# The first two graph pairs of an attention layer, normalised and turned at the end of the layer before it

## The reference

```python
h = jnp.maximum(_layernorm(x, axis=-1), 0.0)
x = x + _L0_gnn_ref(h, adj, ...)      # relation, masked by adj, divided by its norm
h = jnp.maximum(_layernorm(x, axis=-1), 0.0)
x = x + _L1_gnn_ref(h, ..., adj)      # additive attention
h = jnp.maximum(_layernorm(x, axis=-1), 0.0)
x = x + _L2_gnn_ref(h, adj, ...)      # norm_adj @ (h @ weight) + bias
h = jnp.maximum(_layernorm(x, axis=-1), 0.0)
x = x + _L3_gnn_ref(h, adj, ...)      # attention with 8 heads of 32, masked by adj

# _L3_gnn_ref
q = (x @ Wq + bq).reshape(b, n, H, HD)
k = (x @ Wk + bk).reshape(b, n, H, HD)
v = (x @ Wv + bv).reshape(b, n, H, HD)
scores = jnp.einsum('bqhd,bkhd->bhqk', q, k) / jnp.sqrt(jnp.float32(HD))
scores = scores + (1.0 - adj)[None, None, :, :] * -1000000000.0
attn = jax.nn.softmax(scores, axis=-1)
out = jnp.einsum('bhqk,bkhd->bqhd', attn, v).reshape(b, n, d)
return out @ Wo + bo
```

## Time and profile before

| | |
|---|---|
| median of 3 runs | 755.95 us (754.49 to 757.42) |
| profiled execution | 755.72 us |
| its span, first to last instruction | 753.8 us |
| mean granted TensorE clock | 0.989 |
| busy PE | 709.9 us (94%) |
| busy DVE | 627.1 us (83%) |
| busy ACT | 564.8 us (75%) |
| busy POOL | 474.5 us (63%) |

### The profile page before, as it was taken

The page is one execution under the profiler, slowest core; times in us unless marked ns, Lnnn a source line. Parts: engine busy times, 40 slices in busy tenths (PEclk is TensorE's granted clock), DMA queues, the critical chain, the costliest instruction groups (busy, mean ns, idle before and its releaser), DMA issues.

```text
span 753.8 us, 22983 instructions
## 1 busy us (share of the span) xinstructions
PE 709.9 (94%) x6938; PEld 657.7 (87%) x6938; DVE 627.1 (83%) x2650; ACT 564.8 (75%) x1896; POOL 474.5 (63%) x610
## 2 busy tenths in 40 slices
PE   6999999998999999779998999999999999999995
PEld 5999999997777777679997899999999999999984
DVE  5888778776899999869998888888888888888863
ACT  3665655653778787747663899999999999999985
POOL 2445445445678778478884766667666766667652
PEclk9999999999999999879999999999999999999999
DMA  7323300000000000000000000000000000000001
GB/s 233 86 84 86 96 14 0 0 0 1 2 0 2 1 2 0 2 1 0 0 0 1 3 29 28 28 28 14 28 28 28 28 15 28 28 28 28 14 30 43
DMA packets 21682, 20.15 MB, mean 27 GB/s; under 512 B 2432, under 2 KB 21632, under 8 KB 21632
## 3 DMA queue, kind: packets, MB, share of 16 engines
q1 hardware_dynamic: 19440, 18.16, 7.6%
q10 hardware_dynamic: 2192, 1.44, 0.7%
HBM read 11.21 MB, written 8.39 MB: 26 GB/s over the span
## 4 chain that ended last, share of the span: by engine, by line
PE 76%; DVE 16%; issue 4%; ACT 1%; POOL 1%; DMA 1%; DVEq 0%; POOLq 0%; ACTq 0%
PE bank L253 43%; PE bank L1083 7%; PE bank L1075 5%; PE bank L1093 4%; PE bank L323 4%; PE bank L153 4%; PE bank L233 3%; PE bank L333 3%; DVE stats L116 3%; DVE xs L854 2%; DVE masked_e L830 2%; DVE leaky_e L835 2%; DVE att L848 2%; DVE small L838 2%; PE bank L243 1%
## 5 line engine op out<-in xcount | busy, mean ns | idle before, releaser
L1152 ACT ACTIVATE prob<-wide,small 128x128 f32<-128x128 f32 x512 | 199.0, 395 | 20.0 <-DVE small L1236 20.0
L1201 POOL TENSOR_TENSOR prob<-prob,small 128x512 f32<-128x512 f32 x128 | 133.3, 1041 | 104.3 <-DVE small L1250 104.3
L142 POOL TENSOR_TENSOR rstd<-vare,mhalf 128x2 f32<-128x2 f32 x128 | 88.8, 694 | 64.9 <-DVE vare L131 64.9
L1236 DVE CUSTOM_DVE_ANT_0 wide<-bank,mbias 128x128 f32<-128x128 f32 x512 | 116.0, 283 | 9.3 <-PE bank L1075 9.3
L224 POOL TENSOR_SCALAR xn<-xs,nmean,rstd 128x256 f32<-128x256 f32 x186 | 102.4, 561 | 12.8 <-POOL rstd L142 10.8
L116 DVE BATCH_NORM_STATS2 stats<-xs 128x6 f32<-128x256 f32 (+1 forms) x256 | 95.5, 415 | 5.8 <-DMA xs<-in_x_dram 4.7
L1152 ACT ACTIVATION_READ_ACCUMULATOR prob<-wide,small 128x1 f32 x512 | 98.4, 192 | 0.0
L1159 ACT COPY probT<-bank 128x512 f32<-128x512 f32 x128 | 72.1, 588 | 6.3 <-PE bank L1083 5.3
L1083 PE MATMUL bank<-ident,prob 128*128 128x128 f32 x512 | 73.9, 276 | 1.9 <-POOL prob L1201 1.9
L490 POOL TENSOR_TENSOR rnorm<-norm,mhalf 128x2 f32<-128x2 f32 x32 | 22.1, 691 | 79.9 <-ACT relsq L431 79.9
L1083 PEld LDWEIGHTS bank<-ident,prob 128*128 128x128 f32 x512 | 57.0, 140 | 8.9 <-issue 5.9
(11 more groups left out here) (136 smaller groups left out, 1795.9 us busy)
## 6 DMA issues: line engine op xcount, KB each, us to landing
out_dram<-xs SPq DMA_DIRECT2D x32, 256.0 KB, 2.1
xs<-in_x_dram SPq DMA_DIRECT2D x29, 256.0 KB, 2.7
xs<-in_x_dram ACTq DMA_DIRECT2D x1, 512.0 KB, 7.2
xs<-in_x_dram ACTq DMA_DIRECT2D x1, 256.0 KB, 4.0
wq<-in_L_gnn_Wq_dram SPq DMA_DIRECT2D x1, 256.0 KB, 3.6
wk<-in_L_gnn_Wk_dram ACTq DMA_DIRECT2D x1, 256.0 KB, 4.9
wv<-in_L_gnn_Wv_dram SPq DMA_DIRECT2D x1, 256.0 KB, 5.5
w<-in_L_gnn_W_dram SPq DMA_DIRECT2D x1, 256.0 KB, 7.3
```

What stands on the lines that cost most here:

```text
L142: nc.gpsimd.tensor_tensor(rstd[:, b, :], vare[:, b, :], mhalf[:, :], ALU.pow).then_inc(rstd_ready, 1)
L1152: ins = nc.scalar.activation(prob[:, r, i, :], wide[:, r, i, :], ACT.Exp, bias=nmax[r][:, i:i + 1], scale=-1.0, accum_out=rsum[r][:, i:i + 1])
L1201: nc.gpsimd.tensor_tensor(prob[:, r, :, :], prob[:, r, :, :], rinv[r].unsqueeze(2).to_broadcast([128, QUAD, N]), ALU.mult).then_inc(prob_r ...
L1236: nc.vector.tensor_tensor_reduce(out=wide[:, r, i, :], in0=SS[r][:, i * N:(i + 1) * N], in1=mbias[:, :], scale=-1.0, scalar=3e38, op0=ALU. ...
```

## The change

Pairs 0 and 1 of the fourth layer take the third layer's path: moments into the new buffers 2 and 3, root and shift on POOL, relu_norm on ACT into the free tiles neg_u and exp_u[0] (xq). The two tensor_scalar of DVE and POOL's centre of pair 1 go. The moments of pair 1 move into the place of the tensor_scalar. PE turns pair 1 into bank 6 (TQ1), between project_q(0) and project_k(0), in place of TQ behind project_v(0). DVE's low half of pair 1 moves from period 0 (behind its first mask_max) to before it, and the moments of pair 2 move from there to before update(31). Semaphore counts follow, as xn_ready of the fourth layer now counts from pair 2.

```diff
-        stats = sb("stats", [128, 2, 2, 6])
+        stats = sb("stats", [128, 4, 2, 6])
...
+        xq = [neg_u, exp_u[0]]
...
@@ third layer @@
-            YT, OO, TQ = bank[0:2], bank[2:4], bank[7]
+            YT, OO, TQ, TQ1 = bank[0:2], bank[2:4], bank[7], bank[6]
...
-                pe.wait_ge(l3_xn_ready, 1)
-                transposes(TQ).then_inc(l3_tr_done, 1)
+                pe.wait_ge(l3_xq_ready, 1)
+                transposes(TQ, xq[0]).then_inc(l3_tr_done, 1)
                 outputs(PAIRS - 1, 1)
...
                 copy_high(PAIRS - 2, 0)
+                relu_norm(act, 0, 2, xq[0], l3_shift_ready).then_inc(l3_xq_ready, 1)
                 copy_high(PAIRS - 1, 1)
                 act.wait_ge(l3_tr_done, 1)
-                nc.scalar.activation(hT_high, TQ[:, :], ACT.Relu).then_inc(l3_high_ready, 1)
+                nc.scalar.copy(hT_high, TQ[:, :]).then_inc(l3_high_ready, 1)
+                relu_norm(act, 1, 3, xq[1], l3_shift_ready).then_inc(l3_xq_ready, 1)
...
-                inverse_root(pool, 0, l3_stats_ready, l3_rstd_ready)
-                add_bias(PAIRS - 2)
-                add_bias(PAIRS - 1)
-                inverse_root(pool, 1, l3_stats_ready, l3_rstd_ready, 1)
-                pool.wait_ge(yt_done, PAIRS)
-                centre(pool, 1, 1, l3_rstd_ready, l3_xn_ready)
+                for p in range(2):
+                    root_and_shift(pool, p, l3_stats_ready, l3_rstd_ready, l3_shift_ready, 2 + p)
+                    add_bias(PAIRS - 2 + p)
...
                     step(p, p % 2, norms=p + 3 < PAIRS)
-                    if p == PAIRS - 3:
-                        dve.wait_ge(xn_ready, PAIRS - 1)
-                        layer_norm_stats(dve, 0, l3_step, l3_stats_ready)
-                    if p == PAIRS - 2:
-                        dve.wait_ge(l3_rstd_ready, 1)
-                        dve.wait_ge(yt_done, PAIRS - 1)
-                        for g in range(2):
-                            ins = nc.vector.tensor_scalar(xn[:, g, :], xs[:, g, :], mv[:, 0, g, 0:1], rstd[:, 0, g:g + 1],
-                                                          ALU.subtract, ALU.mult)
-                        ins.then_inc(l3_xn_ready, 1)
+                    if p in (PAIRS - 3, PAIRS - 2):
+                        layer_norm_stats(dve, p - PAIRS + 3, l3_step, l3_stats_ready, p - PAIRS + 5)
                 dve.wait_ge(l3_high_ready, 1)
-                nc.vector.scalar_tensor_tensor(hT_low, TQ[:, :], 0.0, hT_high.bitcast(F32), ALU.max,
-                                               ALU.subtract).then_inc(l3_low_ready, 1)
+                nc.vector.tensor_tensor(hT_low, TQ[:, :], hT_high.bitcast(F32), ALU.subtract).then_inc(l3_low_ready, 1)
                 update(PAIRS - 2, 0)
+                dve.wait_ge(xn_ready, PAIRS)
+                layer_norm_stats(dve, 2, l3_step, l3_stats_ready, 0)
                 update(PAIRS - 1, 1)
-                layer_norm_stats(dve, 1, l3_step, l3_stats_ready, 1)
@@ fourth layer @@
...
                 project_q(0)
+                pe.wait_ge(l3_xq_ready, 2)
+                transposes(TQ1, xq[1]).then_inc(tr_done, 1)
                 pe.wait_ge(l2_yt_ready, PAIRS)
                 project_k(0)
                 project_v(0)
-                turn(1, 1)
...
                     if has(p, 0, PAIRS - 1):
-                        relu_high(p + 1)
+                        relu_high(p + 1, TQ1 if isinstance(p, int) and p == 0 else TQ)
...
-                    if has(p, 0, PAIRS - 1):
+                    if has(p, 1, PAIRS - 1):
                         low_h(p + 1)
...
-                dve.wait_ge(xn_ready, 1)
-                layer_norm_stats(dve, 2, dstep, stats_ready, 0)
+                low_h(1, TQ1)
                 period(0, 0)
```

More of the change, by code:

```diff
@@ L61, in gnn_stack_kernel @@
         mhalf = sb("mhalf", [128, 2])
-        stats = sb("stats", [128, 2, 2, 6])
[L63 to L67, removed]
+        stats = sb("stats", [128, 4, 2, 6])
+        mv = sb("mv", [128, 4, 2, 2])
+        vare = sb("vare", [128, 4, 2])
+        nmean = sb("nmean", [128, 4, 2])
+        rstd = sb("rstd", [128, 4, 2])
+        shift = sb("shift", [128, 4, 2])
         xn = sb("xn", [128, 2, D])
@@ L210, in gnn_stack_kernel @@
         l3_stats_ready, l3_rstd_ready, l3_step = sem("l3_stats_ready"), sem("l3_rstd_ready"), sem("l3_dve_step")
+        l3_xq_ready, l3_shift_ready = sem("l3_xq_ready"), sem("l3_shift_ready")
         l3_xn_ready, l3_tr_done, l3_high_ready, l3_low_ready = sem("l3_xn_ready"), sem("l3_tr_done"), sem("l3_high_ready"), sem("l3_low_ready")
@@ L1047, in turn @@
                 def turn(p, b):
-                    pe.wait_ge(xn_ready, p + 1)
+                    pe.wait_ge(xn_ready, p - 1)
                     pe.wait_ge(q_ready, since(p))
@@ L1142, in _, with relu_high @@
             def _(act):
-                def relu_high(p):
+                def relu_high(p, ps=TQ):
                     act.wait_ge(tr_done, p + 1)
                     act.wait_ge(v_done, since(p))
-                    nc.scalar.activation(hT_high, TQ[:, :], ACT.Relu).then_inc(high_ready, 1)
+                    nc.scalar.activation(hT_high, ps[:, :], ACT.Relu).then_inc(high_ready, 1)
                 def exponentials(p, r):
@@ L1194, in add_bias @@
                 def add_bias(p):
-                    pool.wait_ge(xn_ready, p + 1)
+                    if p < 2:
+                        pool.wait_ge(l3_xq_ready, p + 1)
+                    else:
+                        pool.wait_ge(xn_ready, p - 1)
                     nc.gpsimd.tensor_tensor(x_pair(p), x_pair(p), rows[:, 2:3, :].to_broadcast([128, 2, D]),
@@ L1250, in inverse, with low_h @@
                     nc.vector.reciprocal(rinv[r], rsum[r]).then_inc(rinv_ready, 1)
-                def low_h(p):
+                def low_h(p, ps=TQ):
                     dve.wait_ge(high_ready, p + 1)
-                    nc.vector.scalar_tensor_tensor(hT_low, TQ[:, :], 0.0, hT_high.bitcast(F32), ALU.max,
+                    nc.vector.scalar_tensor_tensor(hT_low, ps[:, :], 0.0, hT_high.bitcast(F32), ALU.max,
                                                    ALU.subtract).then_inc(low_ready, 1)
@@ L1288, in period @@
                     if has(p, 0, PAIRS - 3):
-                        dve.wait_ge(xn_ready, p + 2)
+                        if p > 0:
+                            dve.wait_ge(xn_ready, p)
                         moments(dve, p + 3, dstep, 1 - b)
```

## The result

| | before | after |
|---|---|---|
| median, 6 runs each | 755.55 us | 751.65 us |
| profiled execution, its span | 755.72, 753.8 us | 750.46, 748.7 us |
| mean granted TensorE clock, profiled | 0.989 | 0.993 |

The medians are 3.9 us apart. The ratio, taken from all runs, is 0.9945, or 0.55% faster, with a 95% interval of 0.993 to 0.996. In later runs the same kernel took 751.54 us against 755.15 us, ratio 0.9957 (0.9942 to 0.9973).

What follows compares the result with a forecast made beforehand. PE bounds the fourth layer, so earlier project_q(2) is kept. Third layer's end 0.48 us, less 0.44 for the turn, plus 1.10 from the low half gives 1.14 us: 755.95 to 754.81 us, range 752.9 to 756.9 us.

Steps and rivals of the forecast that it cites:

- The reading of the bound: Fourth layer is PE-bound at 10.51 us a period; whatever brings project_q(2) earlier is kept to the end, one for one.
- Part 1: End of the third layer: outputs(31) starts 0.48 us earlier, with the wait for DVE becoming a wait for ACT.
- Part 2: Pair 1's turn between project_q(0) and project_k(0) adds 0.44 us to PE's path; scores(0) keeps its time within 0.04 us.
- Part 3: Moments of pair 2 ahead of update(31): 1.28 us on DVE delay update(31) and copy_q(0), but cost nothing.
- Part 4: low_h(1) before the scores: project_q(1) comes 1.69 us earlier, of which 1.10 us is gained in the first period.
- (a): Fourth layer's first period: nothing of low_h(1)'s move is kept, through a POOL or DVE hold-up; 755.9 us, chance 0.12.
- (d): End of the third layer gains nothing because relu_norm(0) waits 0.5 us longer; 0.66 us saved, 755.3 us, chance 0.18.
- (b): Fourth layer's first period: the whole removed PE gap, 1.69 us, is kept; 754.3 us, chance 0.06.
- PE doesn't wait for xq[1]: Denies the rival that late xq[1] stalls PE between q and k, making the kernel slower: 757.0 us, chance 0.04.
- the term for the loops: Loops outside the border between third and fourth layer: counted as unchanged, the same 10.51 us a period in the fourth.
- rival (e): Something outside the border, in the loops, shifts by several microseconds either way; chance 0.08, half to each side.
- another period: Sign of being wrong: the fourth layer's saturated stretch shows a period other than 10.51 us.

Runs made afterwards that it cites:

- turn_late: Changed kernel with pair 1's turn, still into bank 6, moved back behind project_v(0); low_part(29) to project_q(2) takes 24.75 us instead of 25.20.
- before_front_128: Kernel before with an unused 128-byte tile in front of xs, moving all large tiles, weights too, together; fourth-layer period 10.510 us.

## Why the prediction was wrong

**The reading of the bound** held. PE fills the fourth layer, and what reached project_q(2) early was kept: 4.09 us ahead there, 5.15 us at the last v copy. The 2.4 us of idle PE are those of one window of ten microseconds, though. From 396 to 422 PE is busy 21.44 of 26.00 us, so 4.56 us of idle PE lie at the border, and it isn't so that 3.8 us are "more than all PE idling" there.

**Part 1.** Right in the mechanism, 0.21 us short in size. The place of the wait (ACT's copy behind relu_norm(0)) was forecast; outputs(31) came 0.69 us earlier and not 0.48: counted from low_part(29), relu_norm(0) starts at 3.66 us where I had 3.74, the copy 0.10 us before its end where I had 0.02 behind it, and low_part(31) at 5.25 where I had 5.48. nmean of pair 1 started 0.05 us before the bias addition ended, so it says nothing of a hold-up.

**Part 2.** Right, 0.44 us forecast, 0.45 measured by turn_late. With part 1, scores(0) came 0.33 us earlier and not 0.04, which is nearly all of the 0.31 us by which the border gained more than forecast.

**Part 3.** Right in the cost, nothing waits for it. The times were not: from low_part(29), update(31) starts at 9.14 us (9.08 before, 9.43 by my times), and copy_q(0) at 9.79 us, which is 1.17 us earlier than before (10.96), because the moments of pair 1 no longer stand in front of it.

**Part 4.** Right: 1.12 us from v copy to v copy, 1.10 forecast, and 1.09 us measured by putting it back. PE's next wait was for POOL's division, 0.46 us at 411.00, inside what DVE's chain allows. ACT left more room than I gave it: it still idles 0.61 us ahead of pair 1, where I left 0.16.

**Rivals** (a) to (d) are out: the gain of part 4 is kept, but as 1.09 us and not as the 1.69 us of (b); the end of the third layer gained 0.69 us; PE doesn't wait for xq[1]. nmean under a division took 0.98 us again, as before, and cost what it had cost before.

**The step that failed** is the term for the loops, which the sum puts at nothing ("the same 10.51 us a period") and rival (e) sets aside: "no row speaks for it, the loops' instructions are the same", with a chance of 0.08. The same instructions don't mean the same duration. The first line of the diff, and five like it, enlarge the six statistics tiles, every later tile moves by 128 bytes, and PE's split products run faster there: 0.025 us a pair in the first layer (0.7 us from pair 2 to 30) and 0.035 us a period in the fourth (1.0 us over 29). In the third layer, low_part(6) to low_part(29) takes 55.16 to 55.26 us in the seven profiles at 0 and 54.99 to 55.06 us in the seven at 128, another 0.2 us. That is about 1.9 us, more than the border, from lines that the sum doesn't mention. With 1.45 us of the border it makes 3.4 of the measured 3.6 to 3.9 us. Of the signs of being wrong, "another period" is the one that came.

From the forecast 754.81 us to the measured 751.65 us it is 3.16 us: about 1.9 of the place, 0.31 of the border, 0.40 of the median before, which six runs put at 755.55 and not at 755.95 us, and some 0.55 that aren't accounted for. The range couldn't have held the place's term, and it isn't what its own terms give either: 754.3 - 1.5 is 752.8 and 757.0 + 1.5 is 758.5 us.

**What stays open.** The two first profiles are 5.15 us apart at the last v copy, of which 3.4 us are explained. Most of the rest, 1.04 us, lies between the first layer's update of pair 30 and low_part(4), where the clock falls. There the granted clock is 0.50, the 1.2 GHz level, for some stretches, behind ones in which PE is only partly busy: in the kernel before 1.19 of the 3.00 us from 178.00, and 1.76 of the 3.70 us ahead of 314.70. The kernel before, in four stretches (columns as in rows 1):

```profile
178.00:181.00 3.00, 1.19 (x7) 1.02 (x8) 2.86 (x12) 0.73 (x3) 1.55 (x3) 1.00 0.02 5
181.50:184.50 3.00, 3.00 (x10) 2.18 (x8) 0.47 (x4) 0.59 (x1) 1.12 (x2) 0.51 0.00 0
314.70:321.00 6.30, 4.23 (x17) 4.05 (x18) 4.31 (x13) 4.85 (x11) 2.80 (x4) 0.50 0.00 1
328.50:335.00 6.50, 6.01 (x28) 6.04 (x29) 4.70 (x16) 3.59 (x8) 4.98 (x7) 0.50 0.01 3
```

and the changed one:

```profile
178.00:181.50 3.50, 2.45 (x14) 2.05 (x14) 2.73 (x13) 0.00 (x0) 2.20 (x5) 1.00 0.02 5
181.50:185.00 3.50, 3.19 (x18) 2.36 (x17) 2.01 (x6) 1.09 (x3) 1.38 (x3) 1.00 0.00 0
315.30:318.70 3.40, 3.29 (x15) 3.30 (x16) 2.99 (x10) 2.91 (x6) 1.94 (x2) 0.50 0.01 2
325.50:332.30 6.80, 5.36 (x25) 5.39 (x26) 5.00 (x17) 3.37 (x7) 5.81 (x9) 0.50 0.01 2
```

Over the 18 profiles, that way takes 156.0 to 158.3 us. Its mean is 156.9 us in the five profiles with the old entry to the fourth layer and 156.9 us in the thirteen with the new one. So I take it for chance between executions; that is argued from these profiles, not shown by an experiment. The low clock at about 180 came in all of those five and in six of the thirteen, which the code up to there, the same in all, doesn't explain. With it the way takes 157.3 us in the mean, without it 156.3 us (156.0 to 156.5 in all seven), and of the two first profiles the one before has it and the changed one has not. The timed runs agree: in the later comparison, seven runs of the kernel before had a mean granted clock of 0.993, with spans of 751.6 to 752.0 us, and two of the changed kernel had it, with 748.5 and 748.7 us. At a like clock the change is worth 3.2 us, a little less than the 3.4 us of the sum. One stretch may belong to the change: in before_front_128 the clock fell at the border itself,

```profile
410.00:413.40 3.40, 3.12 (x14) 3.12 (x15) 2.12 (x19) 3.40 (x19) 1.55 (x2) 0.50 0.00 0
```

right where the old order leaves PE idle 1.65 us, and its v copy to v copy took 10.90 instead of 9.53 us. (That is why its border, 28.00 us, isn't compared.) No other profile had it. How often it happens isn't known. What makes the pace depend on the distance modulo 256 bytes is open too.

## What to carry to other kernels

A change to the size of any tile is a change to the place of all tiles behind it; where one engine fills a stage, put its price down as unknown by some tenths of a per cent of that stage (the places tried here lie 0.9% apart in the fourth layer), and separate it by two builds, the old code on the new places and the new code on the old ones. When comparing single profiles, compare intervals between instants inside a stage: at this border they repeat within 0.02 us, while a difference of medians was taken to need 3.8 us. Put a new piece of in-order work where its engine already waits for another: the turn of pair 1 was free behind v and cost 0.45 us in front of k.

## What was unexpected of the hardware

The pace of fp32r split products changes with the places of tiles in SBUF, as far as tried with the distance modulo 256 bytes between the tiles up to the statistics, the weights among them, and those from xn on, h among them: 24 matmuls of q and k took 2.88 us at 0, 2.83 us at 128 and 2.80 us at 192, and a period of the fourth layer between 10.444 us (96) and 10.542 us (160), 0.9%. No distance tried was best for every product: at 96, the best for the fourth layer, the first layer's pair takes 5.138 us against 5.055 us at 32.
